# Twenty-one short series of matmuls behind the last product of a graph layer

## The chip, the cores and the metric

The kernel runs on one core of a Trainium2 chip. The metric is the device time of one execution in microseconds (us). A core has the engines TensorE (in the rows PE, and PEld for its loads of weights), VectorE (DVE), ScalarE (ACT), GpSimd (POOL) and SyncE (SP), and 16 DMA engines between HBM and the on-chip memory.

## The reference

With x of 4096 x 256, adj of 4096 x 4096 and W of 256 x 256, all float32:

```
def _L0_gnn_ref(x, adj, W, b):
    agg = jnp.matmul(adj, x)
    out = jnp.matmul(agg, W.T) + b
    return jax.nn.relu(out)
h = jnp.maximum(_layernorm(x, axis=-1), 0.0)
x = x + _L0_gnn_ref(h, adj, L0_gnn_W, L0_gnn_b)
```

## The kernel before

The output is computed transposed, features on partitions. The 4096 output columns are cut into 4 groups of 1024 (`GW`), each in two chunks of 512 (`BANK`). For each group TensorE goes over the 32 tiles (`TILES`) of 128 neighbours. It multiplies in float32r, and to keep precision every operand is split into a rounded part (`_hi`) and the rest (`_lo`), so a product takes three passes: hi by hi, hi by lo, lo by hi (`PASSES`). Such a tile is 12 matmuls of 128 x 512, written by `add_up` at L379: the stationary operand (the weights) is a 128 x 128 piece of `h_sb`, which holds the normalised x of all tiles, both parts; the moving operand is 512 columns of `adj_hi` or `adj_lo`, which have four buffers each.

For every tile SP loads a piece of adj into `adj_in`, ACT rounds it into `adj_hi` (L313), and DVE subtracts to make `adj_lo` (L223). In the first group ACT, DVE and POOL also make h from x. The sums of a group lie in four of the eight PSUM banks, the next group uses the other four.

When a group is summed, ACT and DVE split the sums into `agg_hi` and `agg_lo` (L347, L283), and `w_product` (L420) multiplies them with `w_hi` and `w_lo`: 24 matmuls per group, placed behind the fourth tile of the next group. For the last group (`LAST`) there is no next group, so its product stands at the end of TensorE's queue. Its fourth piece is cut into two halves of 256 columns, so it is 18 matmuls of 512 columns and 12 of 256. Behind each piece ACT applies bias and relu (L355), DVE adds x (L292) and SP stores the piece (L183). SP then waits for all stores, and the block ends when every engine has come to its end.

At the start, while the first data are still on the way, TensorE runs 11 matmuls (`WARM_UP`, L429) on `warm`, a tile of zeros in bfloat16. The order on each engine is the order in which the code is written; semaphores alone join the engines.

Of the kernel before, what the change touches and what calls it, by code (L numbers as in the profile page):

```python
# [4 lines left out]
P = 128  # L5

def bass_preln_gnn_residual(
# [16 lines left out]
    N, D = x.shape  # L25
    TILES = N // P
    KB = D // P
    BANK = 512
    CHUNKS = 2
    GW = CHUNKS * BANK  # L30
# [21 lines left out]
    with ctx:  # L52
        def sb(name, shape, dt=fp32):
            return ctx.enter_context(nc.sbuf_tensor(name, shape, dt))
# [15 lines left out]
        warm = sb("warm", [P, BANK], mybir.dt.bfloat16)  # L70
        centred = sb("centred", [P, U, D])
        h_sb = sb("h_sb", [P, TILES, 2, D], fp32r)
        adj_in = sb("adj_in", [P, U, GW])
        adj_hi = sb("adj_hi", [P, U, GW], fp32r)
        adj_lo = sb("adj_lo", [P, U, GW], fp32r)
# [5 lines left out]
        banks = [ctx.enter_context(nc.psum_tensor(f"bank{i}", [P, BANK], fp32)) for i in range(2 * SUMS)]  # L81
# [32 lines left out]
        def bank(g, block_, c):  # L114
            return banks[(g % 2) * SUMS + c * KB + block_]
# [3 lines left out]
        def chunk(c):  # L119
            return slice(c * BANK, (c + 1) * BANK)  # L120
# [5 lines left out]
        def made_chunk(t, c):  # L126
            return CHUNKS * t + c + 1

        def made_tile(n):
            return made_chunk(n, CHUNKS - 1) if n < EARLY else CHUNKS * EARLY + n - EARLY + 1  # L130

        def pieces(g):

            whole = [(c, o, 0, BANK) for c, o in GROUP_BANKS]
            if g < LAST:
                return whole
            c, o, _, _ = whole.pop()
            return whole + [(c, o, 0, BANK // 2), (c, o, BANK // 2, BANK)]

        def within(c, a, b):  # L140
            return slice(c * BANK + a, c * BANK + b)

        def product(g, c, o, a, b):

            return bank(g if a == 0 else g + 1, o, c)[:, a:b]

        @block.sync
        def _(sp):
            def load_x(i):
                a, b = X_PIECES[i]  # L150
                sp.dma_start(x_sb[:, a:b, :], x_v[:, a:b, :]).then_inc(s_x[i], 16)

            def load_chunk(t, c):
                sp.dma_start(adj_in[:, t, chunk(c)], adj_v[:, t, chunk(c)]).then_inc(s_early[t][c], 16)

            def load_adj(n):
                g, t = divmod(n, TILES)
                if n >= U:
                    sp.wait_ge(s_hi, made_tile(n - U))
                    sp.wait_ge(s_lo, made_tile(n - U))  # L160
                sp.dma_start(adj_in[:, n % U, :], adj_v[:, t, g * GW:(g + 1) * GW]).then_inc(s_adj[n % U], 16)

            load_x(0)
            load_chunk(0, 0)
            load_x(1)
            load_chunk(0, 1)
            load_chunk(1, 0)
            load_chunk(1, 1)
            load_x(2)
            load_adj(2)  # L170
            load_x(3)
            load_adj(3)
            load_x(4)
            for n in range(U, GROUPS * TILES):
                load_adj(n)
                i = n // 4 + 4
                if n % 4 == 0 and i < len(X_PIECES):
                    load_x(i)

            for i, (c, o, a, b) in enumerate(pieces(LAST)):  # L180
                sp.wait_ge(s_sum, LAST * SUMS + i + 1)
                at = LAST * GW + c * BANK
                sp.dma_start(out_v[:, o, at + a:at + b], out_sb[:, o, within(c, a, b)]).then_inc(s_last[i], 16)  # L183
            for s in s_last:
                sp.wait_ge(s, 16)
            sp.wait_ge(s_out, 16 * LAST)
# [182 lines left out]
        @block.tensor  # L369
        def _(pe):  # L370

            PASSES = ((0, 0), (0, 1), (1, 0))
            adj_parts = (adj_hi, adj_lo)

            def add_up(g, t, chunks, hp, ap):
                n = g * TILES + t
                for kb in range(KB):
                    for c in chunks:
                        last = nc.tensor.matmul(bank(g, kb, c)[:], h_sb[:, t, hp, kb * P:(kb + 1) * P],  # L379
                                                adj_parts[ap][:, n % U, chunk(c)],  # L380
                                                start=(t == 0 and (hp, ap) == (0, 0)),
                                                stop=(hp == 1), skip_group_check=True)
                return last

            def early_tile(t):

                pe.wait_ge(s_hhi, t + 1)
                for c in range(CHUNKS):
                    pe.wait_ge(s_hi, made_chunk(t, c))
                    add_up(0, t, [c], 0, 0)  # L390
                    pe.wait_ge(s_lo, made_chunk(t, c))
                    add_up(0, t, [c], 0, 1)
                    if c == 0:
                        pe.wait_ge(s_hlo, t + 1)
                    last = add_up(0, t, [c], 1, 0)
                last.then_inc(s_pe, 1)

            def sum_tile(g, t, chunks, arrived):
                n = g * TILES + t
                for hp, ap in PASSES:  # L400
                    if not arrived:
                        if (hp, ap) == (0, 0):
                            if g == 0:
                                pe.wait_ge(s_hhi, n + 1)
                            pe.wait_ge(s_hi, made_tile(n))
                        elif ap == 1:
                            pe.wait_ge(s_lo, made_tile(n))
                        elif g == 0:
                            pe.wait_ge(s_hlo, n + 1)
                    last = add_up(g, t, chunks, hp, ap)  # L410
                return last

            def w_product(g):
                for c, o, a, b in pieces(g):
                    pe.wait_ge(s_alo, g * SUMS + (c + 1) * KB)
                    if a > 0:
                        pe.wait_ge(s_relu, g * SUMS)
                    for kb in range(KB):
                        for wp, ap in PASSES:
                            last = nc.tensor.matmul(product(g, c, o, a, b),  # L420
                                                    (w_hi, w_lo)[wp][:, kb, o * P:(o + 1) * P],
                                                    (agg_hi, agg_lo)[ap][:, kb, within(c, a, b)],
                                                    start=(kb == 0 and (wp, ap) == (0, 0)),
                                                    stop=(kb == KB - 1 and wp == 1))
                    last.then_inc(s_prod, 1)

            pe.wait_ge(s_warm, 1)
            for _ in range(WARM_UP):
                nc.tensor.matmul(bank(1, 0, 0)[:], warm[:, 0:P], warm[:], start=True, stop=True)  # L429
            for t in range(EARLY):  # L430
                early_tile(t)
            for t in range(EARLY, TILES):
                sum_tile(0, t, range(CHUNKS), False).then_inc(s_pe, 1)
            pe.wait_ge(s_wlo, 1)
            for g in range(1, GROUPS):
                if g >= 2:

                    pe.wait_ge(s_relu, (g - 1) * SUMS)
                for t in range(TILES if g < LAST else TILES - U):
                    if t == SPLIT_AT:  # L440
                        w_product(g - 1)
                    sum_tile(g, t, range(CHUNKS), False).then_inc(s_pe, 1)
            for c in range(CHUNKS):
                for t in range(TILES - U, TILES):
                    last = sum_tile(LAST, t, [c], c > 0)
                last.then_inc(s_chunk, 1)
            w_product(LAST)

# [22 lines left out]
```

## Time and profile before

| | |
|---|---|
| time before, median of 2 runs | 383.03 us (382.74 to 383.32) |
| the profiled execution's own time | 382.79 us |
| its span, first to last instruction | 381.0 us |
| TensorE busy (share of the span) | 376.3 us (99%) |
| matmuls | 1649 |
| matmuls on the chain that ended last | 99% of the span |

The profile shows one execution on the one core. Its own time is 1.8 us longer than its span. Matmuls overlap in the records: one starts before the one ahead of it is over, so the mean duration of one is not the pace. The pace is the time from start to start, and it is read where many of them follow each other without a wait.

### The profile page before, as it was taken

The numbers are of one execution on the slowest core, as the hardware profiler recorded it, in microseconds if no ns is written. First come the engines' busy times: TensorE is split into PE (matmuls) and PEld (weight loads), VectorE is DVE, ScalarE is ACT, GpSimd is POOL, SyncE is SP. The second block draws the span as 40 slices with busy tenths as digits, with TensorE's granted clock in tenths as the row PEclk, the third lists the DMA queues.
The fourth block names the chain that finished last, engine by engine and source line by source line (L and its number), as shares of the span: only waits on it lengthen the run. The fifth ranks groups of instructions, "written<-read, shape, count | busy, mean of one in ns | idle before, by whom it ended". The sixth has DMA issues, their size and how long they took to land.

```text
span 381.0 us, 4425 instructions
## 1 busy us (share of the span) xinstructions
PE 376.3 (99%) x1649; PEld 308.2 (81%) x1649; DVE 218.1 (57%) x293; ACT 170.9 (45%) x197; POOL 63.0 (17%) x79
## 2 busy tenths in 40 slices
PE   8999999999999999999999999999999999999996
PEld 4888888888888888888888888888888888888885
DVE  5999999994745353535564535353565344444424
ACT  4656655654553434343644343434364334343414
POOL 2787777760010000000001000000000100000000
PEclk9999999999999999999999999999999999999999
DMA  7987778669649565656565856565657675656203
GB/s 235 372 288 263 261 267 268 209 201 321 204 156 348 175 214 175 209 179 209 175 207 184 312 178 210 177 211 173 212 174 209 239 255 181 210 181 205 68 2 110
DMA packets 23062, 80.25 MB, mean 211 GB/s; under 512 B 2496, under 2 KB 3264, under 8 KB 23040
## 3 DMA queue, kind: packets, MB, share of 16 engines
q1 hardware_dynamic: 21024, 72.36, 58.0%
q0 software_dynamic: 2016, 7.60, 5.5%
q8 instruction: 13, 0.21, 0.2%
q14 instruction: 9, 0.07, 0.1%
HBM read 75.76 MB, written 4.19 MB: 210 GB/s over the span
## 4 chain that ended last, share of the span: by engine, by line
PE 99%; DVE 0%; ACT 0%; issue 0%
PE bank L379 92%; PE bank L420 6%; PE bank L429 1%; ACT out_sb L355 0%; DVE out_sb L292 0%; DVE warm L256 0%
## 5 line engine op out<-in xcount | busy, mean ns | idle before, releaser
L379 PE MATMUL bank<-adj_hi,h_sb 128*128 128x512 f32 x1024 | 255.1, 390 | 0.0
L223 DVE TENSOR_TENSOR adj_lo<-adj_in,adj_hi 128x1024 fp32r<-128x1024 f32 x126 | 154.2, 1224 | 138.6 <-ACT adj_hi L313 138.5
L379 PEld LDWEIGHTS bank<-adj_hi,h_sb 128*128 128x128 f32 x1024 | 192.3, 188 | 40.7 <-ACT h_sb L323 0.9
L313 ACT ACTIVATE adj_hi<-adj_in 128x1024 fp32r<-128x1024 f32 x126 | 133.4, 1059 | 160.7 <-PE bank L379 157.4
L379 PE MATMUL bank<-adj_lo,h_sb 128*128 128x512 f32 x512 | 137.9, 389 | 0.0
L379 PEld LDWEIGHTS bank<-adj_lo,h_sb 128*128 128x128 f32 x512 | 96.0, 188 | 20.5 <-DVE adj_lo L228 0.6
L203 POOL TENSOR_TENSOR rstd<-var_eps,minus_half 128x1 f32<-128x1 f32 x32 | 49.5, 1546 | 2.5
L215 POOL DMA_DIRECT2D out_t_dram<-out_sb x3 | 2.2, 723 | 209.7 <-DVE out_sb L292 209.7
L323 ACT ACTIVATE h_sb<-centred,rstd 128x256 fp32r<-128x256 f32 x32 | 16.3, 509 | 24.2 <-POOL rstd L203 24.0
L292 DVE TENSOR_TENSOR out_sb<-out_sb,xt_sb 128x512 f32<-128x512 f32 (+1 forms) x17 | 11.1, 659 | 7.7 <-ACT out_sb L355 7.7
L355 ACT ACTIVATE out_sb<-bank,b_sb 128x512 f32<-128x512 f32 (+1 forms) x17 | 11.3, 664 | 9.2 <-PE bank L420 9.2
L251 DVE SCALAR_TENSOR_TENSOR h_sb<-centred,rstd,h_sb 128x256 fp32r<-128x256 f32 x32 | 15.3, 479 | 0.0
L234 DVE BATCH_NORM_STATS2 stats<-x_sb 128x6 f32<-128x256 f32 x32 | 13.5, 421 | 3.1 <-DMA x_sb<-x_dram 3.1
L283 DVE TENSOR_TENSOR agg_lo<-bank,agg_hi 128x512 fp32r<-128x512 f32 x16 | 10.0, 682 | 7.9 <-ACT agg_hi L347 7.9
L245 DVE TENSOR_SCALAR centred<-x_sb,mean_var 128x256 f32<-128x256 f32 x32 | 13.2, 413 | 1.2
L420 PE MATMUL bank<-agg_hi,w_hi 128*128 128x512 f32 (+1 forms) x34 | 13.0, 381 | 0.0
L420 PE MATMUL bank<-agg_lo,w_hi 128*128 128x512 f32 (+1 forms) x34 | 13.0, 381 | 0.0
L420 PE MATMUL bank<-agg_hi,w_lo 128*128 128x512 f32 (+1 forms) x34 | 13.0, 381 | 0.0
L347 ACT ACTIVATE agg_hi<-bank 128x512 fp32r<-128x512 f32 x16 | 8.3, 596 | 8.7 <-PE bank L379 8.7
L197 POOL TENSOR_TENSOR var_eps<-mean_var,eps_sb 128x1 f32<-128x1 f32 x32 | 6.8, 214 | 23.1 <-DVE mean_var L239 23.1
L420 PEld LDWEIGHTS bank<-agg_lo,w_hi 128*128 128x128 f32 x34 | 6.4, 188 | 1.4
L420 PEld LDWEIGHTS bank<-agg_hi,w_hi 128*128 128x128 f32 x34 | 6.4, 188 | 1.4
(20 smaller groups left out, 31.6 us busy)
## 6 DMA issues: line engine op xcount, KB each, us to landing
adj_in<-adj_t_dram SPq DMA_DIRECT2D x126, 512.0 KB, 3.8
xt_sb<-x_t_dram POOLq DMA_DIRECT2D x4, 1024.0 KB, 7.2
x_sb<-x_dram SPq DMA_DIRECT2D x7, 512.0 KB, 6.5
out_t_dram<-out_sb POOLq DMA_DIRECT2D x3, 1024.0 KB, 5.0
adj_in<-adj_t_dram SPq DMA_DIRECT2D x4, 256.0 KB, 4.3
out_t_dram<-out_sb SPq DMA_DIRECT2D x3, 256.0 KB, 2.0
x_sb<-x_dram SPq DMA_DIRECT2D x4, 128.0 KB, 4.4
w_sb<-w_t_dram POOLq DMA_DIRECT2D x1, 256.0 KB, 5.2
```

The lines of the kernel that those rows point to most:

```text
L203: nc.gpsimd.tensor_tensor(rstd[:, k:k + 1], var_eps[:, k:k + 1], minus_half[:], ALU.pow).then_inc(s_rstd, 1)
L223: nc.vector.tensor_tensor(adj_lo[:, k, :], adj_in[:, k, :], adj_hi[:, k, :].bitcast(fp32), ALU.subtract).then_inc(s_lo, 1)
L234: nc.vector.bn_stats(stats[:, k, :], x_sb[:, t, :]).then_inc(s_stats, 1)
L245: nc.vector.tensor_scalar(centred[:, k, :], x_sb[:, t, :], mean_var[:, k, 0:1], mean_var[:, k, 0:1], ALU.max, ALU.subtract).then_inc(s_cen ...
L251: nc.vector.scalar_tensor_tensor(out=h_sb[:, t, 1, :], in0=centred[:, k, :], scalar=rstd[:, k:k + 1], in1=h_sb[:, t, 0, :].bitcast(fp32), ...
L283: nc.vector.tensor_tensor(agg_lo[:, kb, chunk(c)], bank(g, kb, c)[:], agg_hi[:, kb, chunk(c)].bitcast(fp32), ALU.subtract).then_inc(s_alo, 1)
L292: nc.vector.tensor_tensor(out_sb[:, o, cols], out_sb[:, o, cols], xt_sb[:, o, cols], ALU.add).then_inc(s_sum, 1)
L313: nc.scalar.activation(adj_hi[:, k, :], adj_in[:, k, :], ACT.Copy).then_inc(s_hi, 1)
L323: nc.scalar.activation(h_sb[:, t, 0, :], centred[:, k, :], ACT.Copy, scale=rstd[:, k:k + 1]).then_inc(s_hhi, 1)
L355: nc.scalar.activation(out_sb[:, o, within(c, a, b)], product(g, c, o, a, b), ACT.Relu, bias=b_sb[:, o:o + 1]).then_inc(s_relu, 1)
L379: last = nc.tensor.matmul(bank(g, kb, c)[:], h_sb[:, t, hp, kb * P:(kb + 1) * P], adj_parts[ap][:, n % U, chunk(c)], start=(t == 0 and (hp ...
L420: last = nc.tensor.matmul(product(g, c, o, a, b), (w_hi, w_lo)[wp][:, kb, o * P:(o + 1) * P], (agg_hi, agg_lo)[ap][:, kb, within(c, a, b)] ...
```

## The change

Behind the product of the last group TensorE runs 21 series of 6 matmuls (`REPEAT`), 126 in all, one after the other and without a semaphore. They write into PSUM banks 0 and 1 by turns, which no one reads any more, each with `start=True`. Their operands are tiles that lie in SBUF at that time. All 21 have both operands in float32r except the two with `warm`. Counted from 1 in the order of the calls, they differ in these ways:

- 1 and 21: weights and moving operand as in the sums. 2: the same weights and the same moving operand six times. 3: weights of six different tiles of h. 4: 96 columns of weights.
- 5: weights with a step of two elements. 6 to 9: weights that start 1, 2, 4 and 64 elements further on.
- 10: the moving operand starts 2 elements further on. 11: both do. 12: the moving operand has a step of two elements, 512 columns out of 1024. 13: the moving operand is two runs of 256 columns.
- 14: weights from `adj_hi`. 15: weights from `adj_lo`, and h as the moving operand.
- 16 to 18: 384, 256 and 128 columns of the moving operand.
- 19: both operands bfloat16 (`warm`). 20: bfloat16 and float32r by turns.

```diff
+            REPEAT = 6
+            t = TILES - 1
+
+            def probe(weights, moving, columns=BANK, rows=P):
+                for i in range(REPEAT):
+                    nc.tensor.matmul(banks[i % 2][0:rows, 0:columns], weights(i), moving(i),
+                                     start=True, stop=True)
+
+            def probes():
+                def main(i):
+                    return adj_hi[:, i % 2, 0:BANK]
+
+                def h_cols(i):
+                    kb = i // 2 % KB
+                    return h_sb[:, t, 0, kb * P:(kb + 1) * P]
+
+                probe(h_cols, main)
+                probe(lambda i: h_sb[:, t, 0, 0:P], lambda i: adj_hi[:, 0, 0:BANK])
+                probe(lambda i: h_sb[:, i, 0, 0:P], main)
+                probe(lambda i: h_sb[:, t, 0, 0:96], main, rows=96)
+                probe(lambda i: h_sb[:, t, 0, 0:D:2], main)
+                probe(lambda i: h_sb[:, t, 0, 1:P + 1], main)
+                probe(lambda i: h_sb[:, t, 0, 2:P + 2], main)
+                probe(lambda i: h_sb[:, t, 0, 4:P + 4], main)
+                probe(lambda i: h_sb[:, t, 0, 64:P + 64], main)
+                probe(h_cols, lambda i: adj_hi[:, i % 2, 2:BANK + 2])
+                probe(lambda i: h_sb[:, t, 0, 2:P + 2], lambda i: adj_hi[:, i % 2, 2:BANK + 2])
+                probe(h_cols, lambda i: adj_hi[:, i % 2, 0:GW:2])
+                probe(h_cols, lambda i: adj_hi[:, 0:2, 0:D])
+                probe(lambda i: adj_hi[:, 2, i * P:(i + 1) * P], main)
+                probe(lambda i: adj_lo[:, 2, i * P:(i + 1) * P], lambda i: h_sb[:, t - i, :, :])
+                probe(h_cols, lambda i: adj_hi[:, i % 2, 0:384], columns=384)
+                probe(h_cols, lambda i: adj_hi[:, i % 2, 0:256], columns=256)
+                probe(h_cols, lambda i: adj_hi[:, i % 2, 0:128], columns=128)
+                probe(lambda i: warm[:, 0:P], lambda i: warm[:])
+                probe(lambda i: (warm[:, 0:P], h_sb[:, t, 0, 0:P])[i % 2],
+                      lambda i: (warm[:], adj_hi[:, 0, 0:BANK])[i % 2])
+                probe(h_cols, main)
+
             pe.wait_ge(s_warm, 1)
...
             w_product(LAST)
+            probes()
```

On TensorE, at the end of the program, behind the last two matmuls of the last product (L420), stand now these rows (the first eleven of the added kinds; L433 is the matmul in `probe`):

```order
 L420 MATMUL bank<-agg_lo,w_hi 128x256
 L420 MATMUL bank<-agg_hi,w_lo 128x256
+L433 MATMUL bank<-adj_hi,h_sb 128x512 x18
+L433 MATMUL bank<-adj_hi,h_sb 96x512 x6
+L433 MATMUL bank<-adj_hi,h_sb 128x512 x54
+L433 MATMUL bank<-adj_hi 128x512 x6
+L433 MATMUL bank<-h_sb,adj_lo 128x512 x6
+L433 MATMUL bank<-adj_hi,h_sb 128x384 x6
+L433 MATMUL bank<-adj_hi,h_sb 128x256 x6
+L433 MATMUL bank<-adj_hi,h_sb 128x128 x6
+L433 MATMUL bank<-warm 128x512 x7
```

Nothing ahead of them moved, and the instructions of the other engines are the same as before.

## Rows read from the trace of the kernel before

**Rows 1.** Page, part 1: busy us, share of the span, instructions of each engine.

```profile
PE 376.3 (99%) x1649; PEld 308.2 (81%) x1649; DVE 218.1 (57%) x293; ACT 170.9 (45%) x197; POOL 63.0 (17%) x79
```

**Rows 2.** The chain that ended last, its pieces: start us, us, what.

```profile
0.87 0.28 DVE warm L256
...
1.19 4.87 PE bank L429 x11
6.07 98.81 PE bank L379 x432
104.88 5.59 PE bank L420 x24
110.47 87.05 PE bank L379 x384
...
295.75 76.17 PE bank L379 x336
371.92 5.63 PE bank L420 x30
...
377.57 0.48 ACT out_sb L355
378.05 0.03 issue
378.08 0.43 DVE out_sb L292
```

**Rows 3.** Windows, TensorE: window: us, busy (matmuls), granted clock, DMA share, GB/s.

```profile
120.00:160.00 40.00, 40.00 (x178) 1.00 0.63 203
365.00:371.50 6.50, 6.50 (x30) 1.00 0.01 3
```

**Rows 4.** Timeline of the last product: start us, us, engine, line, what.

```profile
371.75 0.39 PE L420 MATMUL bank<-agg_hi,w_hi 128*128 128x512 f32 x1
371.76 0.19 PEld L420 LDWEIGHTS bank<-agg_lo,w_hi 128*128 128x128 f32 x1
371.99 0.40 PE L420 MATMUL bank<-agg_lo,w_hi 128*128 128x512 f32 x1
...
375.95 0.28 PE L420 MATMUL bank<-agg_hi,w_hi 128*128 128x256 f32 x1
375.96 0.19 PEld L420 LDWEIGHTS bank<-agg_lo,w_hi 128*128 128x128 f32 x1
376.07 0.28 PE L420 MATMUL bank<-agg_lo,w_hi 128*128 128x256 f32 x1
...
377.25 0.28 PE L420 MATMUL bank<-agg_hi,w_lo 128*128 128x256 f32 x1
```

**Rows 5.** Groups by shape: line, engine, operation, shapes, count | busy us, mean ns | idle.

```profile
L379 PE MATMUL bank<-adj_hi,h_sb 128*128 128x512 f32 x1024 | 255.1, 390 | 0.0
L379 PEld LDWEIGHTS bank<-adj_hi,h_sb 128*128 128x128 f32 x1024 | 192.3, 188 | 40.7 <-ACT h_sb L323 0.9
```

**Rows 6.** Timeline of the warm-up's last weight loads (bfloat16).

```profile
4.16 0.15 PEld L429 LDWEIGHTS bank<-warm 128*128 128x128 bf16 x1 [0.28 <-issue]
4.58 0.15 PEld L429 LDWEIGHTS bank<-warm 128*128 128x128 bf16 x1 [0.28 <-issue]
5.01 0.15 PEld L429 LDWEIGHTS bank<-warm 128*128 128x128 bf16 x1 [0.28 <-issue]
```

**Rows 7.** Timeline of the last three stores issued by SP.

```profile
377.60 1.30 SPq L183 DMA_DIRECT2D out_t_dram<-out_sb  x3
```

**Rows 8.** DMA issues from 372 us on: what, queue, count, KB each, us to landing.

```profile
out_t_dram<-out_sb SPq DMA_DIRECT2D x2, 128.0 KB, 2.0
```

## The prediction

> **What bounds the kernel now.** I read the busy shares first: TensorE is busy for 376.3 of 381.0 us, and no other engine passes 57% [rows 1]. A share of busy time alone doesn't say that TensorE sets the end, since its records overlap, so the chain of work that ended last comes next [rows 2]. From 1.19 us to 377.55 us it is TensorE without a break, and only then come one relu of ACT (0.48 us) and one addition of DVE (0.43 us), and behind them the last store. So what is put behind TensorE's last matmul lies beside that short tail as far as the tail reaches, and is the end of the program from there on.
>
> **The pace of a matmul.** Its record lasts 390 ns [rows 5], but that isn't what one more costs. In the sums 384 matmuls take 87.05 us and 336 take 76.17 us [rows 2]: 226.7 ns from start to start in both. In the last product 18 matmuls of 512 columns start from 371.75 to 375.95 us, 4.20 us or 233.3 ns each, and the 11 steps from 375.95 to 377.25 us, of 256 columns, are 118.2 ns each [rows 4]. So there are two paces for 512 columns, 226.7 with weights from h and 233.3 with weights from W, and the operands' place or the order of use is all that tells them apart.
>
> Does the pace depend on the other traffic, which is gone behind the last product? From 120 to 160 us the DMA engines are busy for 0.63 of the time, from 365 to 371.5 us for 0.01 [rows 3], and the piece of the chain that holds the second window has the same 226.7 ns. I take it that the probes keep it too. The granted clock is 1.00 in both windows, and nothing interrupts TensorE between there and the probes, so I leave the clock where it is, at its upper level of 2.4 GHz.
>
> **The change part by part.** It removes nothing and moves nothing. The probes wait for no one, and no one waits for them but the end of the block. The first of them can start one step of 118 ns behind the last matmul of the product, 377.25 + 0.12 = 377.37 us.
>
> Series of 512 columns in float32r: 1 to 15 and 21, 16 series or 96 matmuls. Of 15 of them (90 matmuls) I take 226.7 ns, the pace with weights from h, because weights and moving operands are those of the sums or their neighbours: 20.40 us. Bound: at the pace of the last product it is 90 x 6.6 ns = 0.6 us more.
>
> What about weights that are read in another way (series 4 to 9, 11, 14, 15)? A load of weights starts 0.01 us behind the start of the matmul ahead, and its record lasts 0.19 us, also where matmuls of 256 columns start every 118 ns [rows 4]. So the load itself keeps a pace of 118 ns or better, and the rest of its record is latency. With 512 columns there are 226.7 ns for it. A load that took twice as long would need 236 ns at most, 10 ns over the pace, so I put the odd starts and the step of two at nothing; 48 matmuls by 10 ns, 0.5 us, is the upper bound of that kind. What costs if that cover is gone is a whole load of 188 ns [rows 5], 1.1 us per series.
>
> Series 12 is another matter. Its moving operand has a step of two elements, and a moving operand has no cover: 512 columns at 2.4 GHz take 213.3 ns, and the pace is 226.7, so the stream of float32 is already a little slower than the array's clock. No row shows a strided one. The bounds are 226.7 ns (free) and twice that, 453.4 ns (every second element read is thrown away). I take the second, since a stream that already lags has nothing to spare: 6 x 453.4 = 2.72 us against 1.36.
>
> The narrow ones: 256 columns at 118.2 ns, 6 of them 0.71 us. 384 columns in the middle between 118.2 and 226.7, 172 ns: 1.03 us. 128 columns: half of 118.2 is 59 ns if the columns set it, 118 if the load of weights does; I take 90, 0.54 us, with 0.35 to 0.71 as bounds.
>
> Series 19 in bfloat16: the warm-up's loads of weights start at 4.16, 4.58 and 5.01 us [rows 6], one per matmul, so 0.427 us a matmul. 512 columns in 0.427 us is the lower level, 1.2 GHz, whatever the profile's clock says for these first microseconds. At the upper level it is half, 213 ns: 1.28 us. Series 20, three of each kind: 3 x 213 + 3 x 226.7 = 1.32 us, plus the six changes between the types from there on and into series 19. No row shows a change of type without a wait ahead of it. The bounds are nothing and an exposed load of 188 ns for each, 1.13 us; I take nothing, because a load is 128 columns of something in either type.
>
> The sum: 20.40 + 2.72 + 0.71 + 1.03 + 0.54 + 1.28 + 1.32 = 28.00 us. The last matmul starts a step ahead of 377.37 + 28.00 = 405.37 us and ends 390 - 227 = 163 ns behind that, at 405.53. Then comes the end of the block. Before, the last store is issued at about 378.5 us [rows 7], lands 2.0 us later [rows 8], and 0.5 us are left to the end of the span. Without a landing to wait for I take 0.3 us (bounds 0 and 0.5): a span of 405.8 us. With the 1.8 us that the execution's own time is above its span, that is **407.6 us**. The profiled execution (382.79) is 0.24 us below the median of the runs, so the runs may give 407.8; I don't add that.
>
> What the addition would cost without the tail beside it is 28.0 us; the tail of 3.6 us, from 377.37 to 381.0, hides the first sixteen matmuls, less the 0.5 us that the end costs in any case. So 24.8 us show.
>
> **What the Trainium skill says.** On SBUF there is a rule that speaks against my doubled series. The Trainium skill, SBUF — State Buffer, section SBUF: two separate sides, states that consecutive reads of one 16-byte line run at full bandwidth as long as a line is hit at least twice; a step of two float32 elements hits it twice. By that rule series 12 would take 1.36 us and not 2.72, the result 406.3 us. No row here shows a strided operand, so the trace doesn't decide.
>
> On the pace, the rows show 226.7 ns per matmul of 512 columns over whole groups [rows 2]. The Trainium skill, TensorE: Matmul & The Clock Gate, section Back-to-back issue gap, gives a sustained 131 ns for 512 columns in a stream of loads and matmuls; by it the hundred wide ones would take 9.6 us less. The rows contradict it 720 times over.
>
> **Rivals.** First, the step of two is free, and everything else is as above: 407.6 - 1.36 = 406.3 us (406.24). For it: the weight loads of float32 manage their pace beside the stream, so the memory isn't exhausted. Against it: the stream's lag behind the array.
>
> Second, the lag of 13.4 ns (226.7 - 213.3) comes from the other engines' accesses and goes away when they stop: 90 x 13.4 ns is 1.2 us less, 406.4 us, and with a free step 405.0. Against it stands the equal pace where the DMA engines rest [rows 3].
>
> Third, some loads are exposed: a change of type or an odd start drains the array first. One to three series with 188 ns more per matmul, 1.1 to 3.4 us: 408.7 to 411.0 us. For it: no row shows an odd start or a change of type. Against it: 109 ns of slack between 118 and 227.
>
> Fourth, one form falls out of the fast way of float32r altogether, say at four times the time: 6 x 3 x 226.7 ns is 4.1 us a series; 411.7 us and up.
>
> Fifth, the other side: not slower. The matmuls whose results no one reads are hidden in the tail, which has room for 3.6 us, or 16 matmuls at 226.7 ns. That decides only if the 126 took 11 us or less (3.6 + 7.7, where 7.7 us is 2% of 383), 89 ns each. The narrowest pace in the trace is 118 ns, and for 256 columns. The same result, 383 us, comes if they weren't in the program at all, but they stand in its order. Both together get 0.02.
>
> **How the numbers follow.** Forecast (doubled step, nothing else) 0.42, free step 0.30, no lag 0.05, exposed loads 0.13, a slow form 0.08, not slower 0.02. The likeliest is 407.6. From below the range takes in the free step, 406.3, less 0.5 for the 128 columns and the end, and less 0.3 for the spread of executions: 405.4. From above it reaches into the exposed loads, to 410.6, which leaves some 0.17 out: the slow form, the rest of the exposed loads, no lag with a free step, and not slower. A measurement of this kernel can tell a change of about 2% from none, which is 375.4 to 390.7 us, and every case but the last lies above: slower 0.97, same 0.02, faster 0.01.
>
> **What would show it.** In the timeline of the changed kernel the matmuls of L433 should start at 377.4 us, every 0.227 us, with series 12 at 0.453 and the narrow ones at 0.17, 0.12 and 0.09. The chain that ended last should end in L433 with no ACT or DVE behind it, and everything ahead of 377 us should read as before. The relu, addition and stores of the last pieces should stand where they stood. I am wrong if a gap opens between two series, if the granted clock falls in the probes, or if series 5 to 9 differ from series 1 by more than 10 ns.

## The result and the profile after

The changed kernel takes 408.26 us (408.16 to 408.37, 2 runs) against 383.03 us: a ratio of 1.066, 95% interval 1.0642 to 1.0677. That is slower by 25.2 us. The forecast was 407.6 us and the range 405.4 to 410.6.

The page's first lines after, which answer to [rows 1]:

```profile
span 406.3 us, 4677 instructions
PE 404.4 (100%) x1775; PEld 329.7 (81%) x1775; DVE 218.2 (54%) x293; ACT 170.6 (42%) x197; POOL 63.0 (16%) x79
```

TensorE has 126 matmuls more and 28.1 us more of busy time, and the span is 25.3 us longer. DVE, ACT and POOL have as many instructions as before.

The end of the chain that ended last, after (start us, us, what), which answers to [rows 2]:

```profile
295.76 76.17 PE bank L379 x336
371.93 5.62 PE bank L420 x30
377.55 28.55 PE bank L433 x126
```

The last sums and the last product ahead of the probes are the same to 0.01 us. Then the chain ends in L433, the matmul in `probe`; the relu, addition and store that ended it before are gone from it. They haven't moved, they are covered: in the timeline after, the last relu and the last addition start at 377.59 and 378.09 us, within 0.02 us of where they started before.

```profile
377.59 0.47 ACT L355 ACTIVATE out_sb<-bank,b_sb 128x256 f32<-128x256 f32 x1 [0.23 <-PE bank L420]
...
378.09 0.43 DVE L292 TENSOR_TENSOR out_sb<-out_sb,xt_sb 128x256 f32<-128x256 f32 x1 [0.17 <-ACT out_sb L355]
```

TensorE in the timeline from the product's last matmul on, after:

```profile
377.27 0.28 PE L420 MATMUL bank<-agg_hi,w_lo 128*128 128x256 f32 x1
377.39 19.53 PE L433 MATMUL bank<-adj_hi,h_sb 128*128 128x512 f32 x78
396.75 1.52 PE L433 MATMUL bank<-adj_hi 128*128 128x512 f32 x6
398.11 1.52 PE L433 MATMUL bank<-h_sb,adj_lo 128*128 128x512 f32 x6
399.47 2.56 PE L433 MATMUL bank<-adj_hi,h_sb 128*128 128x384 f32 x18
401.87 1.69 PE L433 MATMUL bank<-warm 128*128 128x512 bf16 x7
403.20 0.58 PE L433 MATMUL bank<-adj_hi,h_sb 128*128 128x512 f32 x1
403.63 0.39 PE L433 MATMUL bank<-warm 128*128 128x512 bf16 x1
403.67 0.58 PE L433 MATMUL bank<-adj_hi,h_sb 128*128 128x512 f32 x1
```

From one row's start to the next: series 1 to 13 take 19.36 us, series 14 and 15 1.36 us each (226.7 ns a matmul), the three narrow series 2.40 us together. No row has idle time ahead of it, and the granted clock of this stretch is 1.00. In the window of series 14 and 15 DVE, ACT and POOL have 0.00 us of busy time, and the DMA engines stand still (window: us, then busy of PE (matmuls), granted clock, DMA share, GB/s):

```profile
396.80:399.40 2.60, 2.60 (x13) 1.00 0.00 0
```

So the question isn't whether the probes lie on the path, but what each form costs, and why most of the first thirteen series aren't at 226.7 ns: with 2.72 us for the step of two (below) the other 72 matmuls share 16.64 us, 231 ns each. By the starts of the single matmuls in this trace only series 9 (weights 256 bytes on) and nearly series 3 (227.3) have the pace of the sums; series 2 and 4 are at 230 to 231 ns, and 1, 5 to 8, 10, 11 and 13 at 231 to 234.

### The profile page after: what moved, and what is told of

It is laid out like the page before. It is cut to its first block, busy times and chain, and to the rows that moved or that the text cites. A ratio compares the mean times of both kernels' runs of the same rounds, so it can differ in the third digit from the quotient of the medians.

```text
span 406.3 us, 4677 instructions
## 1 busy us (share of the span) xinstructions
PE 404.4 (100%) x1775; PEld 329.7 (81%) x1775; DVE 218.2 (54%) x293; ACT 170.6 (42%) x197; POOL 63.0 (16%) x79
## 4 chain that ended last, share of the span: by engine, by line
PE 98%; DMA 1%; DVE 0%; SPq 0%; issue 0%
PE bank L379 86%; PE bank L433 7%; PE bank L420 6%; DMA x_sb<-x_dram 1%; DVE adj_lo L228 0%; DVE stats L234 0%; SPq L154 0%; DVE centred L245 0%; SPq L151 0%; DVE mean_var L239 0%
## 5 line engine op out<-in xcount | busy, mean ns | idle before, releaser
L433 PE MATMUL bank<-adj_hi,h_sb 128*128 128x512 f32 (+4 forms) x105 | 25.0, 395 | 0.0
L433 PEld LDWEIGHTS bank<-adj_hi,h_sb 128*128 128x128 f32 (+1 forms) x105 | 18.9, 188 | 5.1 <-issue 1.5
L420 PE MATMUL bank<-agg_hi,w_hi 128*128 128x512 f32 (+1 forms) x34 | 13.0, 381 | 0.0
L420 PE MATMUL bank<-agg_lo,w_hi 128*128 128x512 f32 (+1 forms) x34 | 13.0, 381 | 0.0
L420 PE MATMUL bank<-agg_hi,w_lo 128*128 128x512 f32 (+1 forms) x34 | 13.0, 381 | 0.0
```

The source lines that it names most:

```text
L420: last = nc.tensor.matmul(product(g, c, o, a, b), (w_hi, w_lo)[wp][:, kb, o * P:(o + 1) * P], (agg_hi, agg_lo)[ap][:, kb, within(c, a, b)] ...
L433: nc.tensor.matmul(banks[i % 2][0:rows, 0:columns], weights(i), moving(i), start=True, stop=True)
```

## The experiments

Nine kernels. Four of them (the first, second, sixth and seventh) put long series behind the last product, every series on two lines of its own, so that the chain gives its pace. In those the probes are part of the chain to its end. Each of these four ran once, so their paces are compared inside one trace; the granted clock is 1.00 in all of them. The others are compared with runs of the kernel before that were taken beside them (median 382.68 or 382.83 us). None of the nine leaves out a part of the computation.

### The same 21 series, each 24 long

```diff
+                for i in range(0, 6):  # series 1
+                    nc.tensor.matmul(banks[i % 2][0:128, 0:512], h_sb[:, t, 0, i // 2 % KB * P:(i // 2 % KB + 1) * P], adj_hi[:, i % 2, 0:512], start=True, stop=True)
+                for i in range(6, 24):  # series 1
+                    nc.tensor.matmul(banks[i % 2][0:128, 0:512], h_sb[:, t, 0, i // 2 % KB * P:(i // 2 % KB + 1) * P], adj_hi[:, i % 2, 0:512], start=True, stop=True)
...
```

> The same 21 series as in the change, each 24 matmuls long instead of 6, in the same order, every series on lines of its own (6 and then 18 matmuls), so that the chain gives the pace of each. In two series the six tiles are gone over again. It tells what belongs to a form from what belongs to the place in the queue. Theory A (the form and the place of the operands set the pace): series 1 and 21, which are the same calls, have one pace in their last 18; the step of two stays at 0.45 us, 128 columns at 0.11, bfloat16 at 0.216. Theory B (a disturbance is left over for some matmuls and dies out): every series of 512 plain columns settles at 0.2267 us in its last 18, whatever its start offset, and only the first six differ. Sum by A: 24/6 x 28.3 = 113 us behind 377.4, a time of about 493 us; by B about 2 us less.

It took 493.76 us. Pieces of the chain: L434 is series 1, L446 series 4 (96 columns of weights), L462 series 8 (weights 16 bytes on), L476 and L478 series 12 (step of two), L502 series 18 (128 columns), L506 series 19 (bfloat16), L510 series 20 (by turns), L514 series 21.

```profile
379.22 4.10 PE bank L434 x18
...
395.58 4.15 PE bank L446 x18
...
417.84 4.20 PE bank L462 x18
...
438.65 2.72 PE bank L476 x6
441.37 8.16 PE bank L478 x18
...
473.55 2.01 PE bank L502 x18
...
476.87 3.88 PE bank L506 x18
...
482.12 4.14 PE bank L510 x18
...
487.65 4.08 PE bank L514 x18
```

Both theories are half right. Series 21, the same calls as series 1, settles at 4.08 us for 18, 226.7 ns, and series 1 comes to 4.10: what they had more in the change, means of 230 and 234 ns, is a disturbance that dies out. By single starts series 1 is at 226.7 ns from its 11th matmul on. Series 8 stays at another pace, 4.20 us is 233.3 ns. So there is a pace that belongs to the placement, and a left-over behind a change of form. But placement isn't all: series 4 has the starts of series 2 and only 96 columns of weights, and stays at 230.6 ns; series 5 has weights with a step of two, and stays at 233. The step of two is 453.3 ns, 128 columns 111.7 ns, bfloat16 215.6 ns, and two matmuls of different types 460 ns.

### Thirty-two placements

```diff
...
+                for i in range(0, 8):  # series 2
+                    nc.tensor.matmul(banks[i % 2][0:128, 0:512], h_sb[:, t, 0, 2:P + 2], adj_hi[:, 0, 0:512], start=True, stop=True)
...
```

> Behind the last product of the kernel before, 32 series of 8 and then 24 matmuls, all with the same weights and the same moving operand throughout a series: weights that start 0, 2, 4, 8, 16, 32, 48 and 64 elements into a piece of h, by moving operands that start 0, 2, 4 and 8 elements into adj_hi. If the pace hangs on where the two operands lie to each other (theory A), the same difference of starts gives the same pace: 2 with 2, 4 with 4, 8 with 8 are as 0 with 0, 0.2267 us, and some differences are at 0.231 to 0.234. If it hangs on the start of each alone, rows and columns of the table differ, not the diagonals. If it is only a left-over disturbance (theory B), all last 24 are at 0.2267. Time by B 377.4 + 1024 x 0.2267 + 2 = 612 us, up to 7 us more by A.

It took 617.08 us, inside the 612 to 619 that both theories span. Pieces of the chain for the 24 later matmuls of six series: weights 0, 16, 192 and 256 bytes on with the moving operand at its start, then both 8 and both 32 bytes on.

```profile
379.24 5.45 PE bank L434 x24
...
393.94 5.60 PE bank L442 x24
...
423.73 5.49 PE bank L458 x24
...
431.05 5.44 PE bank L462 x24
...
445.82 5.54 PE bank L470 x24
...
579.71 5.45 PE bank L542 x24
```

The chain has the 32 later pieces; divided by 24 they are, in ns (starts in bytes):

| moving \ weights | 0 | 8 | 16 | 32 | 64 | 128 | 192 | 256 |
|---|---|---|---|---|---|---|---|---|
| 0 | 227 | 230 | 233 | 233 | 233 | 232 | 229 | 227 |
| 8 | 233 | 231 | 233 | 233 | 234 | 233 | 235 | 233 |
| 16 | 232 | 233 | 231 | 237 | 230 | 233 | 231 | 232 |
| 32 | 233 | 231 | 228 | 227 | 233 | 234 | 233 | 233 |

Theory A holds for 0 and 32 bytes: with the same start, or 256 bytes apart, 227, and elsewhere 1 to 10 ns more. It fails for 8 and 16 bytes, where equal starts give 231. The distance counts, but it isn't the whole of it: the good pace came only where both operands start with their tile or a multiple of 32 bytes on. Which of the two starts matters no run tells, since at equal distance both move together. No placement is faster than 226.7.

### The W tiles moved by 32 bytes

```diff
+        pad_ahead = sb("pad_ahead", [P, 8])
         w_sb = sb("w_sb", [P, KB, D])
         w_hi = sb("w_hi", [P, KB, D], fp32r)
         w_lo = sb("w_lo", [P, KB, D], fp32r)
+        pad_behind = sb("pad_behind", [P, 56])
```

> The kernel before without any probe; the three tiles of W are moved by 32 bytes and all tiles behind them by 256 bytes. Where the place of the weights decides (theory A), the last product's pace falls from 233.3 to 226.7 ns and each of the first three products from 5.59 to 5.44 us; 90 matmuls by 6.6 ns is 0.6 us, and the time 382.4 us. Where the order of use decides (theory C: both passes write one PSUM bank six times in a row in the product, and alternate in the sums), nothing changes, 383.0 us.

With the second padding all tiles behind W move by 256 bytes, which leaves what exceeds multiples of 256 as it was. The time is 381.95 us against 382.68 for the kernel before: a ratio of 0.9981, interval 0.9972 to 0.999. The chain in its middle, as in [rows 2]:

```profile
109.93 87.04 PE bank L381 x384
196.97 5.44 PE bank L422 x24
```

The product takes 5.44 us instead of 5.59 us, and the sums are unchanged. Order of use (theory C) is refuted: the product still writes one bank six times in a row, at 226.7 ns. This kernel is 0.7 us faster than the kernel before, and the interval leaves out 1; 0.15 us in each of three products and 0.11 in the last are 0.56 of it. Two tiles of padding buy that.

### All tiles behind those of W moved by 32 bytes

```diff
         w_lo = sb("w_lo", [P, KB, D], fp32r)
+        pad_behind = sb("pad_behind", [P, 8])
```

> The kernel before without any probe; the tiles of W stay and all tiles behind them, h, adj and agg among them, are moved by 32 bytes, so that both kinds of operands start at a multiple of 64 bytes. If the start itself decides (a multiple of 64 is bad for weights), the sums fall to the pace of the product: 1536 x 6.6 ns = 10 us more, 393 us. If the distance between the two operands decides and only its rest by 64 bytes counts, the sums stay and the product gains 0.6 us: 382.4. If its rest by 256 bytes counts, nothing changes: 383.0. By theory C (order of use) nothing changes either.

382.45 us against 382.68, ratio 0.9991, interval 0.9982 to 1.0: the time alone can't be told from no change, so the chain has to decide.

```profile
111.46 87.04 PE bank L380 x384
198.50 5.49 PE bank L421 x24
```

### h and adj moved apart

```diff
         h_sb = sb("h_sb", [P, TILES, 2, D], fp32r)
+        pad_behind = sb("pad_behind", [P, 8])
         adj_in = sb("adj_in", [P, U, GW])
```

> The kernel before with every tile behind h_sb moved by 32 bytes, and nothing else: the weights of the sums and their moving operands are then apart as those of the last product were in the kernel before (32 bytes off a multiple of 256). If this distance sets the pace, the 1536 matmuls of the sums go from 226.7 to 233.3 ns: 10.2 us more, 392.9 us; the products, whose distance changes to 64 bytes off such a multiple, go from 233.3 to 228.9, 0.4 us less. Together 392.5 us. If the order of use or the start of each tile alone decides, the time is 382.7.

392.81 us against 382.83, ratio 1.0264, interval 1.0249 to 1.0279.

```profile
113.00 89.59 PE bank L380 x384
202.59 5.50 PE bank L421 x24
```

384 matmuls of the sums take 89.59 us instead of 87.05, 233.3 ns each. The product, now 192 bytes apart as in the kernel ahead, takes 5.50 us for its 24, 229.2 ns. Thirty-two unused bytes cost 10 us, 2.6%; 392.5 was foreseen from the distances. Here and in the two kernels ahead the same instructions run in the same order on the same data; only addresses differ.

### Forms and widths

```diff
...
+                for i in range(6, 24):  # series 1
+                    nc.tensor.matmul(banks[i % 2][0:128, 0:256], h_sb[:, t, 0, 0:P], adj_hi[:, 0, 0:512:2], start=True, stop=True)
...
```

> Behind the last product of the kernel before, 19 series of 6 and then 18 matmuls, each with fixed operands. (1 to 5) float32r, 256 columns, with a step of 2, 3 and 4 elements, in pairs of two neighbours with two left out, and plain: if the price is that of a read of 8 bytes of which only 4 are used, steps 2, 3 and 4 cost alike, about 0.227 us, and the pairs cost as the plain ones, 0.118; if it is the stretch of memory gone over, step 4 costs 0.45 and the pairs 0.227. (6 to 9) bfloat16, 256 columns with a step of 2 (4 bytes) and plain, 128 columns with a step of 4 (8 bytes) and plain: by bytes the step of 2 is free, 0.109 us; by the step it is 0.216. (10, 11) bfloat16 with 96 columns of weights, 512 and 128 moving columns: whether the load is then slower, and whether it shows. (12 to 15) 128 moving columns by 128, 96, 64 and 32 columns of weights in float32r: if the load sets the 112 ns, the pace falls in proportion, 0.084 and then 0.056. (16, 17) 512 moving columns by 64 and 32 columns of weights: if the 13 ns above 213.3 come from the reading of weights beside the stream, they shrink, to 0.220 and 0.217; if they are the stream's own, they stay at 0.227. (18) types by twos: if a change of type costs 9 ns, as the 460 ns for two in the change's series 20 against 216 + 227 suggest, four matmuls take 904 ns. (19) plain, 0.2267.

Pieces of the chain for the later 18 of each: L434 and L442 steps of two and four (the step of three, L438, has 4.08 us); L446 pairs; L450 plain, all 256 columns; L454 and L458 bfloat16 with a step of two and plain; L462 bfloat16, 128 columns with a step of four, L466 plain.

```profile
378.82 4.14 PE bank L434 x18
...
389.80 4.20 PE bank L442 x18
...
395.37 4.08 PE bank L446 x18
...
400.17 2.16 PE bank L450 x18
...
403.02 2.04 PE bank L454 x18
...
405.72 1.97 PE bank L458 x18
...
408.37 2.09 PE bank L462 x18
...
410.80 1.00 PE bank L466 x18
```

For 256 columns of float32r: 230, 227, 233 and 227 ns, against 120 plain. The stretch of memory doesn't count, since a step of four costs what a step of two does. In bfloat16 a step of two costs 113 against 109, and a step of four 116 against 56 for 128 columns. So the price follows bytes: elements 4 bytes apart are nearly free, elements 8 or more apart cost about 0.9 ns each. A read of 8 bytes every 0.885 ns (226.7 / 256) is an estimate. It comes within 6% of the steps of both types and of plain float32r (113 ns against 120), but not of the pairs, which I had expected at 118 ns and which take 227.

The loads, in the same chain: 128 moving columns by 128, 96, 64 and 32 columns of weights (L478, L482, L486, the same 1.08 us as L490, and L490), then 512 moving columns by 64 (L494, 4.13 us) and 32 (L498), types by twos (L502), where the expectation of 904 ns for four matmuls meets 913:

```profile
419.00 2.01 PE bank L478 x18
...
421.52 1.53 PE bank L482 x18
...
424.85 1.08 PE bank L490 x18
...
432.84 4.17 PE bank L498 x18
...
438.37 4.11 PE bank L502 x18
```

112, 85, 60 and 60 ns: with 128 and 96 columns of weights the load sets the pace, 0.87 to 0.89 ns a column, and from 64 down the 128 moving columns do. With 512 moving columns fewer weights don't help at all: 229 and 232 ns, more than the 227 of 128 columns from the same start. So the 13 ns above 213.3 (one column a clock at 2.4 GHz; bfloat16 takes 215.6) aren't paid for the number of weights read. In bfloat16 the load goes faster, since 128 by 128 takes 56 ns. By twos, types cost 228 ns a matmul against a mean of 221: some 14 ns a change, and not the 9 that I had carried over from the series by turns, so the price isn't one constant.

### Runs, and the distance in finer steps

```diff
...
+                for i in range(6, 24):  # series 3
+                    nc.tensor.matmul(banks[i % 2][0:128, 0:256], h_sb[:, t, 0, 0:P], adj_hi[:, 0, 0:512].rearrange("p (a b) -> p a b", b=8)[:, :, 0:4], start=True, stop=True)
...
```

> Behind the last product of the kernel before, 19 series of 6 and then 18 matmuls with fixed operands. (1 to 6) float32r, 256 columns: plain, and in runs of 2, 4, 8, 16 and 64 neighbours with as many left out behind each. If a read takes 16 bytes at once and half of them are thrown away for a run of two, runs of 4 and more cost as plain ones, 0.120 us; if any pattern of more than one run is slow, all stay at 0.227, though the change's series 13 (two runs of 256) was not; if the end of a run has a price, it falls in steps from 0.227 towards 0.120. (7, 8) bfloat16 in pairs, 256 columns, and with a step of three (6 bytes), 128 columns: 0.109 and 0.056 if the pitch within 4 bytes or a little over is free, 0.22 and 0.116 if not. (9 to 16) 512 plain float32r columns, weights 32, 64, 96, 128, 160, 192, 224 and 256 bytes further on: the pace by the distance of the two operands, 0.233 at 32 and 224, 0.229 at 192, 0.2267 at 256. (17 to 19) both 64 bytes on: 0.2267; both 16 bytes on: 0.231, as in the table of placements; the moving operand 256 bytes on: 0.2267, as for the weights.

Runs of two and of four neighbours (L438, L442), bfloat16 with a step of three (L462), the weights 256 bytes on (L494), both operands 64 bytes (L498) and 16 bytes on (L502), in the chain:

```profile
381.63 4.15 PE bank L438 x18
...
386.48 2.12 PE bank L442 x18
...
400.51 1.59 PE bank L462 x18
...
442.58 4.08 PE bank L494 x18
...
448.05 4.10 PE bank L498 x18
...
453.54 4.20 PE bank L502 x18
```

Runs of four cost 118 ns for 256 columns, as plain ones, with half of the memory skipped; runs of 8, 16 and 64 do as well (2.16 us each). The cliff is between runs of 16 bytes and runs of 8. Bfloat16 with 6 bytes from element to element is at 88 ns for 128 columns, between 57 for 4 bytes (half of 113) and 116 for 8. By distance in bytes, paces in ns: 233 at 32, 64, 128 and 160 bytes, 234 at 96, 229 at 192, 233 at 224, 226.7 at 256. Both operands 64 bytes on come to the good pace too. Both 16 bytes on gave 233 here and 231 in the table: this placement has more than one settled pace, and which it takes is open.

### Fifteen matmuls only

```diff
+                for i in range(0, 15):
+                    nc.tensor.matmul(banks[i % 2][0:128, 0:512], h_sb[:, t, 0, i // 2 % KB * P:(i // 2 % KB + 1) * P], adj_hi[:, i % 2, 0:512], start=True, stop=True)
```

> The kernel before with only 15 matmuls of the sums' kind behind the last product, 3.5 us of TensorE. If the last relu, addition and store cover what TensorE does in that time, they end at 377.4 + 3.5 + 0.2 = 381.1 in the span, beside 381.0: 382.7 to 382.9 us, no difference that can be told. If the end of the block waits for TensorE in some way that has a price of its own, up to 3.5 us more, 386.2.

382.79 us against 382.83, ratio 1.0, interval 0.999 to 1.0009.

```profile
377.29 3.46 PE bank L432 x15
```

The chain does end in the fifteen, at 380.75 us, but the span is 381.0 as before: they take the place of the store's end, and the time doesn't change.

### The change without the step of two

```diff
-                probe(h_cols, lambda i: adj_hi[:, i % 2, 0:GW:2])
```

> The changed kernel without series 12, the one whose moving operand has a step of two. If the time is the plain sum of what TensorE does, 2.70 us go (its start-to-start time in the changed kernel): 408.26 - 2.7 = 405.6 us. If the step is free and its record misleads, 1.36 us go: 406.9.

405.25 us (405.13 to 406.23), ratio 1.0592 to the kernel before, interval 1.0576 to 1.0608.

```profile
377.52 25.83 PE bank L433 x120
```

The probes take 25.83 us instead of 28.55, 2.72 us less, and the spans of the two profiled executions are 2.7 us apart (406.3 and 403.6). The medians differ by 3.0 us, over two and four runs taken at different times; the 0.3 us beyond the series are not explained.

## Why the prediction came out as it did

The structure held at every step. TensorE sets the end, nothing ahead of 377 us changed, the probes start at 377.39 us (377.37 predicted), and the tail hides what fits into it: 15 matmuls cost nothing, and of the 28.55 us of the change 25.3 us show. The fifth rival is dead by its own mechanism: the cover is real but 3.3 us long.

- **Ninety plain or nearly plain matmuls at 226.7 ns, 20.40 us.** This term was too small, and it is the largest error. Series 14 and 15 were at 226.7. Series 1 to 11 and 13 took 16.64 us where 72 x 226.7 is 16.32. By single starts some 0.17 us of that are the place (series 6 to 8, 10, 11), 0.06 the weights of 96 columns and with a step of two (series 4, 5), and 0.11 settling (series 1, 2, 3, 13); against that series 12 takes 2.70 us by its starts and not 2.72. For the two paces of the kernel before, the prediction named "the operands' place or the order of use" without following it up: moving tiles alone turned the product's 233.3 into 226.7 and the sums' 226.7 into 233.3, so it is the place. It put odd starts at nothing with 10 ns as the bound, and that bound held: the largest settled value of a series here is 233.3. (It counts 48 such matmuls; the series it lists are nine, 54 matmuls, and series 10, with the moving operand off its start, is not among them and is as slow as any.) But the argument under it, that a load hides behind the stream, explains nothing of these 7 ns, since with a quarter of the weights the pace is no better. What in the reading of the two operands makes the pace hang on their distance is open.
- **Settling.** Not foreseen: behind a change of form a good placement needs some matmuls to come to its pace, ten for series 1 of the long series. The six matmuls of the short series 1 and 21 all lie in that stretch.
- **The step of two, 2.72 us.** Measured 2.72. No row bore on it, and with 0.42 against 0.30 the choice of the upper bound was partly luck. The whole time doesn't test it either: with a free step the kernel would have taken about 406.9 us, also inside the range. The kernel without the series tests it. The reason, a stream that already lags has nothing to spare, fits the later series: a step of three in 256 columns and plain reading of 512 both take 226.7 ns, by the estimate above 256 reads of 8 bytes; the pairs don't fit it. The first rival, a free step, would have left 1.36 us.
  The Trainium skill, SBUF — State Buffer, section SBUF: two separate sides, has it that two hits per 16-byte line suffice. The runs contradict it for float32r: a step of two and pairs hit every line twice and run at half rate, 227 to 230 ns for 256 columns against 120.
- **The narrow ones, 2.28 us together.** 2.40 measured. 128 columns are set by the load, 112 ns and not 90; I had the two bounds and no row between them.
- **Bfloat16, 1.28 us, and the turns, 1.32 us.** 215.6 ns instead of 213 and 460 ns for two instead of 440. A change of type has a price of 9 ns by turns, (460 - 226.7 - 215.6) / 2, and some 14 by twos, not the exposed load of 188 ns of the third rival.
- **No lag when the others rest.** The second rival fell: from 396.8 to 399.4 us no engine but TensorE is busy and the DMA share is 0.00, and series 14 and 15 still take 226.7 ns.
- **The slow form**, the fourth rival, didn't occur. No float32r form here took more than twice its plain time.
- **The end.** The last matmul ends at 406.10 us by the chain, the span at 406.3: 0.2 us, where 0.3 was taken.

In sum the probes took 28.55 us against 28.00 predicted, and the whole came out 0.7 us above the forecast. Of the 0.55 us, the first thirteen series are 0.32, the narrow ones 0.12, and bfloat16, the changes of type and series 21 together 0.11. The shorter end took 0.1 us back, and the rest is in the second decimals: the execution's own time was 1.86 us above its span and not 1.8, and the median 0.1 us above that execution.

## What to carry to other kernels

Read TensorE's pace from start to start over many matmuls, and compare two places that should be alike: 226.7 against 233.3 ns in one trace was the sign that 32 bytes of padding were worth 0.7 us here, or 10 us lost if they fall in the wrong place. For float32r keep weights and moving operand a multiple of 256 bytes apart and start both with their tiles or a multiple of 32 bytes on (0, 32 and 64 were good, and the moving operand alone 256 bytes on, at 227 ns in the last series of the run on runs; 8 and 16 were not), and don't feed it a float32 pattern whose runs are shorter than 16 bytes. Work put behind the last matmul is free only as long as the last evacuation and store last, here 3.3 us, and then costs its full pace.

## What was not expected of the hardware

- The pace of a float32r matmul depends on the distance of its two operands in the memory: 226.7 ns at a multiple of 256 bytes, 228.8 at 192, about 233 at most others. Why, no run shows.
- Pairs of float32 neighbours with two left out cost 227 to 230 ns for 256 columns, as single ones do, while bfloat16 pairs (4 bytes in 8) cost 113. A read of 8 bytes explains the second and not the first. Open.
- In series by turns, the float32r matmul's record starts 0.04 us behind that of the bfloat16 one and lasts 0.58 us (timeline after, 403.63 and 403.67 us). The record of a single matmul is no measure of its cost there; the pair is.
